# A mixture-of-LoRA layer on one core: pairs of batches mixed in one go, y moved through DRAM, partial products added by VectorE

## The reference, cut to what matters

```python
W = weights[condition]                          # one 64x64 matrix per batch, 64 batches
y = einsum('bct,bcd->bdt', x, W)                # mix the 64 channels of a batch
gate_logits = einsum('bsd,ed->bse', y, gate_w)  # 8 experts, the top 2 are kept, softmax
result = einsum('bsd,od->bso', y, base_w) + base_b
low = einsum('bsd,erd->ebsr', y, lora_A)        # rank 16
lora_out = einsum('ebsr,eor,bse->bso', low, lora_B, w_full)
return x + result + 2.0 * lora_out
```

## Time and profile before

| | us |
|---|---|
| median of 2 runs | 865.1 (864.77 to 865.43) |
| time of the profiled execution | 868.42 |
| its span in the profile | 866.6 |
| PE / DVE / POOL / ACT busy | 563.1 / 487.9 / 373.4 / 251.2 |
| mean granted TensorE clock | 0.798 of full speed |

### The profile page before, as it was taken

How to read it: one execution, slowest core, us unless ns; L and a number is a source line. 1 busy time by engine, 2 the same in 40 slices (tenths; PEclk the granted TensorE clock), 3 DMA queues, 4 the chain that set the end, 5 groups by cost and what they waited for, 6 DMA issues and landing times.

```text
span 866.6 us, 8835 instructions
## 1 busy us (share of the span) xinstructions
PE 563.1 (65%) x2588; PEld 540.3 (62%) x2588; DVE 487.9 (56%) x582; ACT 251.2 (29%) x356; POOL 373.4 (43%) x280
## 2 busy tenths in 40 slices
PE   9523756857567575665866468675675776568777
PEld 9423745857467575665866468665664766468776
DVE  6934954645556475365844556465464754557252
ACT  6303321233322333213332222333123332223210
POOL 1641724436244372343734245362443724246262
PEclk9766867887779877787877878887797878878788
DMA  9221212211222112221211212112221212211111
GB/s 356 82 79 32 81 53 73 60 42 58 85 73 66 42 74 61 73 73 36 101 41 64 84 50 83 41 72 69 73 68 41 97 40 69 82 29 54 45 59 61
DMA packets 46386, 61.09 MB, mean 70 GB/s; under 512 B 18466, under 2 KB 37026, under 8 KB 46370
## 3 DMA queue, kind: packets, MB, share of 16 engines
q1 hardware_dynamic: 46226, 60.37, 21.3%
q10 hardware_dynamic: 144, 0.52, 0.2%
HBM read 26.25 MB, written 18.87 MB: 52 GB/s over the span
## 4 chain that ended last, share of the span: by engine, by line
SPq 32%; DVE 27%; issue 14%; PE 13%; DMA 8%; ACT 4%; POOL 1%; DVEq 0%; POOLq 0%; ACTq 0%
SPq L318 31%; PE acc L912 11%; DMA y_moved<-y_sum 6%; DVE y_sum L702 5%; DVE x_parts L696 4%; DVE below L740 4%; ACT y_sum L554 4%; DVE y_turned L713 3%; DVE y_lo L719 2%; DVE ties L745 1%; DVE ties L738 1%; DVE s_lo L726 1%; DVE res L789 1%; PE mixed L950 1%; DMA r_raw<-in_w_plain 1%
## 5 line engine op out<-in xcount | busy, mean ns | idle before, releaser
L912 PE MATMUL acc<-r_hi,y_hi 128*128 128x392 f32 x256 | 103.3, 403 | 113.9 <-DVE res L789 113.9
L950 PE MATMUL mixed<-x_parts,w_sel 128*128 128x512 f32 x120 | 53.0, 532 | 182.0 <-DVE y_sum L702 182.0
L702 DVE TENSOR_TENSOR y_sum<-mixed,y_sum 64x1024 f32<-64x1024 f32 x60 | 73.3, 1221 | 163.2 <-ACT y_sum L554 162.3
L950 PEld LDWEIGHTS mixed<-x_parts,w_sel 128*128 128x128 f32 x120 | 25.4, 244 | 190.7 <-issue 190.7
L912 PEld LDWEIGHTS acc<-r_hi,y_hi 128*128 128x128 f32 x256 | 59.0, 231 | 119.4 <-issue 94.6
L554 ACT COPY y_sum<-mixed 64x1024 f32<-64x1024 f32 x60 | 60.5, 1008 | 230.5 <-DMA y_moved<-y_sum 171.8
L425 POOL TENSOR_TENSOR res<-res,snaps 128x768 f32<-128x768 f32 x15 | 27.5, 1834 | 226.4 <-ACT snaps L590 226.4
L713 DVE STREAM_TRANSPOSE y_turned<-y_moved 128x512 f32<-128x512 f32 x60 | 38.9, 683 | 128.9 <-DMA y_moved<-y_sum 128.9
L696 DVE TENSOR_TENSOR x_parts<-x_sb,x_parts 64x1024 fp32r<-64x1024 f32 x60 | 101.0, 1683 | 1.9
L920 PE MATMUL acc<-t_hi,s_hi 128*128 128x384 f32 x240 | 99.8, 416 | 0.0
L912 PE MATMUL acc<-r_lo,y_hi 128*128 128x392 f32 x256 | 99.8, 391 | 0.0
(11 more groups left out here) (92 smaller groups left out, 1165.7 us busy)
## 6 DMA issues: line engine op xcount, KB each, us to landing
x_sb<-in_x SPq DMA_DIRECT2D x32, 512.0 KB, 3.3
out<-res SPq DMA_DIRECT2D x31, 512.0 KB, 2.7
y_moved<-y_sum SPq DMA_DIRECT2D x480, 32.0 KB, 1.8
t_raw<-in_w_quads SPq DMA_DIRECT2D x3, 768.0 KB, 10.5
scratch<-low_turns SPq DMA_DIRECT2D x16, 128.0 KB, 1.9
low_turns<-scratch SPq DMA_DIRECT2D x64, 32.0 KB, 1.8
r_raw<-in_w_plain SPq DMA_DIRECT2D x8, 196.0 KB, 5.3
res<-in_x_first SPq DMA_DIRECT2D x2, 512.0 KB, 5.2
```

Of the source, the lines that this page charges most:

```text
L702: nc.vector.tensor_tensor(part, mixed[i % 2 * CH:(i % 2 + 1) * CH, :, :], part, ALU.add) \
L912: return nc.tensor.matmul(acc[:, i, 0:NP], y_part[:, i, k, :], w_part[:, k, :], start=(k == 0 and product == 0), stop=(k == KT - 1 and pro ...
L950: last = nc.tensor.matmul(mixed[:, h, :], w_sel[:, i % 2, :], x_parts[:, i % 2, h * 512:(h + 1) * 512], start=True, stop=True)
```

## The change

The four mixes of a batch in a step become two mixes of a pair. The operand now holds both batches on 128 rows, with separate high and low tiles, and GpSimd places both batches' matrices on the diagonal of a 128 by 128 matrix, high and low. A mix is then three products for each half of the columns, summed in PSUM, and y comes out whole: ScalarE copies it to `y_whole` in two halves (`y_copy`), and nothing is left to add for VectorE.

`move` writes the two halves to DRAM (`y_scratch`), waits for each to land, and reads it back in the new order with four DMAs of 128 KB: 6 DMAs in the place of 16. In SyncE's step `move(0)` now comes ahead of the loads of x.

VectorE takes the sums S1 to S4 and all four of their low parts, and adds C22 from PSUM to `res` itself (`take`), so `snap` and the three adds on GpSimd are gone. The next product on C22 now waits for `taken`. On VectorE `finish_tails` comes after the second pair's `y_low` and the last `take`.

```diff
             def move(j, u, i):
-                s = 2 * j + u
-                sp.wait_ge(sum_done, 4 * s + 2 * i + 2)
-
-                if u > 0 or i > 0:
-                    sp.wait_ge(turned, 4 * s + 2 * i)
-                for g in range(QUARTERS):
-                    for q in range(QUARTERS):
-                        sp.dma_start(y_moved[q * SQ:(q + 1) * SQ, g, :, :].rearrange("m k a -> m (k a)"),
-                                     y_sum[g * SQ:(g + 1) * SQ, q * RUN:(q + 1) * RUN]).then_inc(moved[i], 16)
+
+                s = 2 * j + u
+                for h in range(2):
+                    sp.wait_ge(y_copied, 4 * s + 2 * i + h + 1)
+                    half = slice(h * (T // 2), (h + 1) * (T // 2))
+                    sp.dma_start(y_scratch[i, :, half], y_whole[:, half]).then_inc(y_out[h], 16)
+                for q in range(QUARTERS):
+                    if q % 2 == 0:
+                        sp.wait_ge(y_out[q // 2], 16 * (2 * s + i + 1))
+                    sp.dma_start(y_moved[q * SQ:(q + 1) * SQ, :, :, :].rearrange("m g k a -> m g (k a)"),
+                                 y_scratch[i].rearrange("(g m) (q r) -> q m g r", g=QUARTERS, q=QUARTERS)[q]) \
+                        .then_inc(moved[i], 16)
...
+            def y_copy(j, u, i):
+                s = 2 * j + u
+                for h in range(2):
+                    act.wait_ge(mix_done, 4 * s + 2 * i + h + 1)
+                    if u > 0 or i > 0:
+
+                        act.wait_ge(y_out[h], 16 * (2 * s + i))
+
+                        act.wait_ge(turned, 4 * s + 2 * i)
+                    nc.scalar.copy(y_whole[:, h * (T // 2):(h + 1) * (T // 2)], mixed[:, h, :]).then_inc(y_copied, 1)
...
+            def take(j, u, n, product, pair, lo, hi):
+
+                s = 2 * j + u
+                dve.wait_ge(prod_done, 7 * s + product)
+                dve.wait_ge(bias_added, 2 * s + pair + 1)
+                if n == 3:
+
+                    dve.wait_ge(taken, 4 * (s - 1) + 2)
+                part = res[:, pair, lo:hi].rearrange("p (b m) -> p b m", m=BW)
+                whole = acc[:, C22:C22 + 1, 0:BW].broadcast_to([P, (hi - lo) // BW, BW])
+                nc.vector.tensor_tensor(part, whole, part, ALU.add).then_inc(taken, 1)
...
             def step(j, u, ahead=True, split=True):
-                s_low(j, u, S2)
-                if ahead:
-                    add_rest(j, u, 0)
-                s_low(j, u, S4)
-                if ahead:
-                    x_low(j, u, 2)
+                make_sums(j, u)
+                for a in (S2, S3, S4, S1):
+                    s_low(j, u, a)
+                if ahead:
+                    x_low(j, u, 1)
                 rank_gates(j, u)
-                if ahead:
-                    add_rest(j, u, 1)
+                take(j, u, 0, 1, 0, 0, BW)
                 apply_gates(j, u)
                 if ahead:
-                    x_low(j, u, 3)
-                    add_rest(j, u, 2)
                     turn(j, u, 0)
-                if split:
-                    x_low(j, u, 4)
-                if ahead:
                     y_low(j, u, 0, 0)
                     y_low(j, u, 0, 1)
-                    add_rest(j, u, 3)
+                take(j, u, 1, 3, 0, BW, 2 * BW)
+                if split:
+                    x_low(j, u, 2)
                 lowT_low(j, u)
-                if split:
-                    x_low(j, u, 5)
+                take(j, u, 2, 5, 1, 0, 2 * BW)
                 if ahead:
                     turn(j, u, 1)
+                    y_low(j, u, 1, 0)
+                    y_low(j, u, 1, 1)
+                    take(j, u, 3, 7, 0, BW, 2 * BW)
                 finish_tails(j, u)
                 if ahead:
                     finish_pair(j, u, 0)
-                    y_low(j, u, 1, 0)
                     finish_pair(j, u, 1)
-                    y_low(j, u, 1, 1)
...
             def mix(j, u, i):
...
+                n = 4 * j + 2 * u + i
+                pe.wait_ge(x_split, n + 1)
+                pe.wait_ge(sel_ready, 2 * n + 2)
                 for h in range(2):
-                    last = nc.tensor.matmul(mixed[:, h, :], w_sel[:, i % 2, :], x_parts[:, i % 2, h * 512:(h + 1) * 512],
-                                            start=True, stop=True)
-                last.then_inc(mix_done, 1)
+                    if u > 0 or i > 0:
+
+                        pe.wait_ge(y_copied, 2 * (n - 1) + h + 1)
+                    for m, (w_part, x_part) in enumerate(((0, 0), (1, 0), (0, 1))):
+                        last = nc.tensor.matmul(mixed[:, h, :], w_sel[:, i, w_part, :],
+                                                x_parts[:, x_part, h * 512:(h + 1) * 512], start=(m == 0), stop=(m == 2))
+                    last.then_inc(mix_done, 1)
```

More of the change, by code:

```diff
@@ L42, in adaln_ffn_kernel @@
     scratch: bass.AP,
+    y_scratch: bass.AP,
 ):
@@ L208, in adaln_ffn_kernel @@
         sel_ready = sem("sel_ready")
-        rest_ready = sem("rest_ready")
-        sum_done = sem("sum_done")
+        mix_done = sem("mix_done")
+        y_copied = sem("y_copied")
+        y_out = [sem(f"y_out{h}") for h in range(2)]
         moved = [sem(f"moved{i}") for i in range(2)]
@@ L337, in step @@
                         store(j, u - 1, i)
+                if ahead:
+                    move(j, u, 0)
                 if load:
@@ L449, in _ @@
                     .then_inc(first_lower, 1)
+            pool.wait_ge(first_lower, 2)
+            for i in range(2):
+                for h in range(2):
+                    nc.gpsimd.tensor_copy(w_sel[:, i, h, :], zeros).then_inc(sel_zero, 1)
             pool.wait_ge(cw_ready, 2)
+            pool.wait_ge(sel_zero, 4)
             select(0, 0, 0)
@@ L475, in _ @@
             add_bias(0, 0, 1)
-            select(0, 0, 4)
-            select(0, 0, 5)
+            pool.wait_ge(bias_added, 2)
+            select(0, 0, 2)
             def t_low(n, a):
@@ L486, in step @@
             def step(j, u, ahead=True, split=True):
-                make_sums(j, u)
+                s = 2 * j + u
                 if ahead:
-                    select(j, u, 2)
-                s_low(j, u, S3)
-                s_low(j, u, S1)
+                    if u == 1:
+                        pool.wait_ge(t_ready_pool, 1)
+                    else:
+                        pool.wait_ge(bias_added, 2 * s)
+                    select(j, u, 1)
                 add_bias(j, u, 0)
@@ L535, in x_high @@
             def x_high(j, u, i):
[L537 removed]
+                n, c = 4 * j + 2 * u + i, 2 + 2 * u + i
                 act.wait_ge(x_in[slot(c)], 16 * (j + c // 4 + 1))
[L539 to L555 removed]
+                if u > 0 or i >= 1:
+                    act.wait_ge(mix_done, 2 * n)
+                nc.scalar.copy(x_parts[:, 0, :], x_sb[:, slot(c), :]).then_inc(x_hi_ready, 1)
+            def y_copy(j, u, i):
+                s = 2 * j + u
+                for h in range(2):
+                    act.wait_ge(mix_done, 4 * s + 2 * i + h + 1)
[3 more added lines that the diff above has]
+                    nc.scalar.copy(y_whole[:, h * (T // 2):(h + 1) * (T // 2)], mixed[:, h, :]).then_inc(y_copied, 1)
             def gate_exp(j, u):
@@ L582, in s_high @@
                     nc.scalar.copy(s_hi[:, a, :, :], s_raw[:, a, :, :]).then_inc(s_hi_ready, 1)
-            def snap(j, u, n, product):
-                s = 2 * j + u
-                act.wait_ge(prod_done, 7 * s + product)
-                if n == 0 and u > 1:
-                    act.wait_ge(snaps_added, 3 * (s - 1))
-                nc.scalar.copy(snaps[:, n, :], acc[:, C22, 0:BW]).then_inc(snapped, 1)
             r_high(0)
@@ L647, in step @@
                     y_high(j, u, 0, 1)
-                if not ahead:
-                    snap(j, u, 2, 5)
+                    y_copy(j, u, 1)
+                if split:
+                    x_high(j, u, 2)
                 lowT_high(j, u)
-                if ahead:
-                    rest(j, u, 3)
-                if split:
-                    x_high(j, u, 5)
-                if ahead:
-                    snap(j, u, 2, 5)
-                snap(j, u, 3, 7 if ahead else 6)
                 if ahead:
@@ L691, in x_low @@
             def x_low(j, u, i):
[L693 to L703 removed]
+                dve.wait_ge(x_hi_ready, 4 * j + 2 * u + i + 1)
+                nc.vector.tensor_tensor(x_parts[:, 1, :], x_sb[:, slot(2 + 2 * u + i), :],
+                                        x_parts[:, 0, :].bitcast(F32), ALU.subtract).then_inc(x_split, 1)
             def turn(j, u, i):
@@ L834, in _ @@
             apply_gates(0, 0)
-            add_rest(0, 0, 0)
-            x_low(0, 0, 2)
-            add_rest(0, 0, 1)
             dve.wait_ge(lb_hi_ready, 1)
@@ L840, in _ @@
                 .then_inc(lb_ready, 1)
-            x_low(0, 0, 3)
+            x_low(0, 0, 1)
             lowT_low(0, 0)
-            add_rest(0, 0, 2)
             turn(0, 0, 0)
@@ L1036, in step @@
```

(2 more changed lines are left out.)

219 lines of the change are left out of this document (69 added, 150 removed).

## The result

The changed kernel takes **528.0 us** (median of 2 runs, 527.5 to 528.5) against 865.1: a ratio of 0.610, 95% interval 0.608 to 0.613. The direction was forecast, the size was not: 587 us with a range of 540 to 690. The profiled execution has a span of 526.5 us against 866.6 and a mean granted TensorE clock of 0.974 against 0.798.

The account below looks back on a forecast made before the run. It took SyncE's issuing of the moves' DMAs, 31% of the chain, as the bound. Forecast: first step 70 + 14 x 34.5 + last step 35 = 588 us of span, less 1.5: 587 us, range 540 to 690.

Parts of the forecast that it names:

- to 31.5 I add 3 us, a tenth, for waits that a walk leaves out: Each middle step: 3 us added to the summed durations for uncounted waits, making 34.5 us a step.
- The walk's own 31.5: One new step built from row durations, following whichever list is latest, from one finish_tails end to the next: 31.5 us.
- rival C: DRAM trips dearer and VectorE's list blocking, with the whole lock of 5.75 on top: 41 us a step, 685 us; chance 0.22.
- Gates done: VectorE's list up to the gates: 12.8 us of work, 4.8 waiting for GpSimd, 0.8 for handovers; done at 18.4 us.
- The lock by the skill: Ports VectorE and GpSimd share: exclusive lock, so VectorE waits 4.8 us for two add_bias; with only shared bandwidth, near 0.
- First move: First half's y through DRAM: 5.2 us instead of 11.9, landing at about 14.5, hidden behind VectorE until 18.4.
- Ranks' trip: SyncE in turn_low after the gates: issue 0.5, landing 1.9, four reads 1.76, given as 3.7 us.
- Second move: Second half's y through DRAM after the ranks' trip: 5.2 us, landed at 27.3 us.
- End of the step: After the second move lands: turn, y_high, last y_low, take and finish_tails 3.9 us, handovers 0.3, ending at 31.5.
- PE's pause of 3 us and its start at the lower level: PE idle some 3 us at step's end, then at lower clock: first 24 matmuls 6.3 us, PE's floor 30.6 a step.
- First step: First step falls from 88.2 us to 70, bounds 66 and 78; add_bias about 6 us earlier, move ahead of x loads 10.
- Rival B: PE becomes the bound: gates at 16.4 as stores end later or sums precede add_bias, step 30.6, total 527 us; chance 0.16.

Follow-up runs that it names:

- experiment 4: Changed kernel with GpSimd's add_bias cut to 128 of its 1024 columns, x and bias missing from the others: 502.1 us, ratio 0.581.
- experiment 5: Changed kernel with VectorE's order alone altered, only S2's s_low ahead of the gates and the other three later, nothing left out: 509.0 us, ratio 0.589.
- experiment 9: Changed kernel with SyncE's old order put back, the two loads of x issued ahead of the first move: 549.9 us, ratio 0.634.
- Experiment 3: Changed kernel with 16 of the 168 matmuls of a step left out, low-part products of S4 with B22 and S1 with T1: 530.8 us, ratio 0.614.

## Why the prediction was wrong

The difference is 588 - 526.5 = 61.5 us of span: 7.3 in the first step (70 against 62.65), 50.2 in the middle (14 x 34.5 = 483 against 432.8), 3.9 in the last (35 against 31.1).

**The step that failed is "to 31.5 I add 3 us, a tenth, for waits that a walk leaves out".** No row stood behind it, and it is 14 x 3 = 42 of the 61.5 us. The walk's own 31.5 was 0.6 above the mean step of 30.9, 8 us in all; 587 less 42 is 545, within 4% of the result. The waits that it was to cover did not come. That the walk came so near is in part luck: against a typical step of 30.3 its gates were 2.1 too late, its second move 1.4 too short and the rest 0.6 too long. The allowance counted twice: the handovers were in the walk (0.8 and 0.3), and the room for bad luck was in rival C. It also set the range, whose lower end of 540 lay above the 538 that the bare walk gives with the first step as measured. Point by point, times from the end of `finish_tails`:

- *Gates done: 18.4 forecast, 16.3 measured* (299.82 - 283.56). The lock was sized about right: 4.8 forecast, 4.1 in the rows (6.81 less four times 0.68), 4.0 by experiment 4. It had one owner, `s_low`: `add_bias` started at 4.0, where 4.3 was forecast, and the sums, over at 4.3, ran free. The other 1.4 of the 2.1 are the 0.8 booked for handovers and 0.6 of small excess: the rows of one engine overlap a little (the sums start 1.65 after `finish_tails`, where 1.9 was booked for the two `finish_pair`).
- *The lock by the skill.* Of VectorE's four operations with two SBUF inputs the two that met an `add_bias` took 2.70 and 2.88 us, the last 0.78; in experiment 4 the four together took 2.84. The Trainium skill (SBUF — State Buffer, Who interferes with whom) calls the ports an exclusive lock; these rows agree. What page and prediction leave open is what the lock costs at the end of a step: it holds VectorE for 4.0 us, but taking it away gives 1.7 (experiment 4), and the order of experiment 5 reaches the same step of 28.8 us with 3.6 of it still there.
- *First move: lands at 14.5, hidden.* The reads are issued from 8.2 to 10.0 and take 2.7: about 12.7, and `turn` does not wait. Hidden, as forecast, with 3.5 us of room, though the landing is 1.8 earlier than forecast; experiment 9 uses the room up and pays at once.
- *Ranks' trip: 3.7 forecast, 3.5 measured* (299.85 to 303.31). The prediction's three terms, 0.5 + 1.9 + 1.76, make 4.2; its 3.7 is right because the landing is counted from the issue, which holds the 0.5 already.
- *Second move: 5.2 forecast, 6.6 measured* (303.43 to 310.01), the one term that was too small: a read of 128 KB into 32 partitions lands in 2.7, where I took 2.0 between 1.8 and 3.3, and the four reads are issued one after the other, in 1.74, where I counted one issue. The Trainium skill (DMA: Bandwidth & Descriptors, Anatomy of one DMA) gave an estimate of 2.6 + 2.3 for a write and a read; measured are 2.1 + 2.7. Its sum of 4.9 is nearer than mine of 4.2, its parts are the other way round. The page fits DMAs that GpSimd issues; these are issued by SyncE. The move landed at 26.4 instead of 27.3.
- *End of the step: 4.2 forecast, 3.8 measured* (310.01 to 313.85).
- *PE's pause of 3 us and its start at the lower level:* wrong. The pause was 1.0 to 1.1 us here and the granted clock 1.00; at 13 of the last 14 starts of a step 24 matmuls took 4.5 us. The prediction's own terms leave no 3 us: with the 2.6 of the LoRA products behind the seventh product PE was busy until 30.6 of a step of 31.5. Measured, the seventh product ends at 309.9, and the LoRA products then stop only for the last `take`. So 24 matmuls take 4.5, not 6.3, and PE's floor is 28.8 (experiment 5), not 30.6. The floor was mis-sized by the price of a pause that another term of the same sum had created.
- *First step: 70 forecast, 62.65 measured,* below my lower bound of 66. Without the selects `add_bias` starts at 39.35 and is done 9 us earlier than before, where I took 6; the first move, at 30.5, no longer waits for it at all.
- *The signs it named:* VectorE the largest share, `s_low` above 2 us beside `add_bias`, `below` near 0.2, each move under 7 us and PE above 75% came true. Steps of 32 to 38 us and landings at 14 to 16 and 27 to 29 did not (30.3, 12.7 and 26.4).

**Rival B named the right time (527) for the wrong reason.** It wanted gates at 16.4 (16.3 measured) because VectorE escapes the lock, which held it for 4.1 us; a step of 30.6 (30.3 to 30.9); and PE as the bound. In its sum a first step 3.4 and a last step 2.9 too long make up for 14 steps that are 0.3 too short: that is luck. Experiment 3 takes 2.8 us of work a step away from PE and gains nothing. The chain still runs through VectorE and the second move; PE's true floor is 1.5 us lower and is reached in kernels 4 and 5.

**Where the 337 us come from**, adding up single parts in the order of the experiments: the move 148 (716.6), the pair's mix with the orders and two low parts 176 (540.5), sums and adds of C22 on VectorE 12 (528.0). Within this the order on SyncE is worth 22 in the new kernel; in the old one, together with the earlier release of `rest`, it cost 6. The prediction gave the second part no line of its own: it counted the new step whole, from its own rows.

## What to carry to other kernels

An allowance "for what was left out" is a term like any other: if no row carries it, put it into the range and not into the sum. When a change frees an engine, recompute what depended on its pauses, the clock above all. And when two engines look nearly level, the busy share does not name the bound: a kernel with a little less work on one of them does, and changing only the order on the other, so that what others wait for comes first, may be worth more (19 us here) than moving work off it (nothing here).
